# Layer 1's rows by scatter and its weights awaited apart; layer 0's index table in one-pass products

## The reference

```python
logits = xf @ W_router + expert_bias
top_vals, top_idx = jax.lax.top_k(logits, K_ACTIVE)
rw = jax.nn.softmax(top_vals, axis=-1)
g_r = silu(xf @ Wg_r[e]); u_r = xf @ Wu_r[e]
out_e = (g_r * u_r) @ Wd_r[e]
out = shared_out + sum_e combine[:, e] * out_e
```

## Time and profile before

| | |
|---|---|
| median of 3 runs | 1096.08 us (1094.7 to 1098.9) |
| profiled execution, its own time | 1098.63 us |
| its span, first to last instruction | 1096.5 us |
| PE busy | 92% of the span |
| mean granted clock of PE, of 2.4 GHz | 0.978 |
| routing of layer 0, from the logits' transposes to the first gate/up products | 338.1 to 363.8 us |
| routed blocks of layer 0, first gate/up to last down | 363.8 to 522.0 us |
| shared products of layer 1 | 704.3 to 759.3 us |
| routed blocks of layer 1, first gate/up to last down | 760.6 to 1061.3 us |
| shared down products | 1061.3 to 1092.3 us |

### The profile page before, as it was taken

One profiled execution on the slowest core, in us unless ns is written; L12 is line 12 of the kernel. 1 busy time (PEld: TensorE's weight loads), 2 busy tenths in 40 slices (PEclk: granted clock), 3 DMA queues, 4 the chain that ended last, 5 costly groups with the idle time before them and its releaser, 6 DMA issues.

```text
span 1096.5 us, 13333 instructions
## 1 busy us (share of the span) xinstructions
PE 1014.0 (92%) x4501; PEld 593.7 (54%) x4502; DVE 527.2 (48%) x934; ACT 323.0 (29%) x482; POOL 384.8 (35%) x333
## 2 busy tenths in 40 slices
PE   6998999999995799999598899999999999999998
PEld 3755555555453466665456555586544554555554
DVE  4466687887576255554565776851111111111114
ACT  2524545554631122221325554511111111111100
POOL 5514676767630222221524775311011111111014
PEclk9999999999997799999799999999999999999999
DMA  4679508000047176411434202503144444410015
GB/s 140 154 233 311 120 1 192 1 1 1 1 142 261 40 264 233 144 57 44 122 101 114 58 2 102 216 4 121 56 158 158 158 172 158 153 33 29 15 34 161
DMA packets 49722, 122.42 MB, mean 112 GB/s; under 512 B 6657, under 2 KB 23945, under 8 KB 49416
## 3 DMA queue, kind: packets, MB, share of 16 engines
q1 hardware_dynamic: 41224, 96.31, 27.8%
q0 software_dynamic: 8448, 25.44, 7.3%
HBM read 87.78 MB, written 22.94 MB: 101 GB/s over the span
## 4 chain that ended last, share of the span: by engine, by line
PE 75%; DVE 11%; DMA 6%; ACT 3%; issue 3%; POOL 1%; SPq 0%; DVEq 0%; ACTq 0%; POOLq 0%
PE PS L1863 22%; PE PS L1884 10%; PE PS L1644 5%; PE PS L1695 5%; PE PS L1554 5%; PE PS L1834 5%; DMA Wd<-in_Wd_r 5%; DVE nmax_part L1256 3%; PE PS L1676 3%; PE PS L1783 3%; PE PS L1910 3%; PE PS L1678 3%; DVE exp_acc L1288 2%; PE PS L1872 2%; DVE nmax L1256 2%
## 5 line engine op out<-in xcount | busy, mean ns | idle before, releaser
L1863 PE MATMUL PS<-Wgu,xbT 128*128 x690 | 287.5, 559 | 10.2 <-DMA Wd<-in_Wd_r 6.5
L1863 PEld LDWEIGHTS PS<-Wgu,xbT 128*128 128x128 f32 x690 | 128.6, 192 | 129.9 <-issue 117.2
L1056 ACT ACTIVATE expS<-PS 128x1024 f32<-128x1024 f32 (+3 forms) x156 | 135.6, 878 | 117.2 <-PE PS L1678 116.0
L953 POOL DMA_DIRECT2D block_rows_out<-yb x46 | 26.5, 576 | 388.2 <-DVE yb L1486 265.7
L1884 PE MATMUL PS<-Wd,hidT 128*128 x414 | 142.5, 490 | 1.5 <-DVE hidT L1448 0.8
L882 POOL TENSOR_TENSOR exp_acc<-exp_acc,expS 128x512 f32<-128x512 f32 (+1 forms) x65 | 124.7, 1918 | 47.3 <-ACT expS L1056 46.6
L1256 DVE TENSOR_REDUCE nmax_part<-PS 128x1 f32<-128x512 f32 x160 | 103.7, 685 | 44.7 <-PE PS L1644 44.0
L1676 PE MATMUL PS<-QA,KS 128*128 128x512 f32 (+3 forms) x312 | 114.3, 372 | 5.5 <-ACT QB L1034 4.8
L1644 PE MATMUL PS<-KS,QA 128*128 128x512 f32 (+2 forms) x288 | 109.5, 425 | 10.0 <-DVE nmax L1256 5.1
L1678 PE MATMUL PS<-QB,KS 128*128 128x512 f32 (+3 forms) x312 | 109.8, 358 | 0.0
L1884 PEld LDWEIGHTS PS<-Wd,hidT 128*128 128x128 f32 x414 | 78.4, 191 | 57.1 <-issue 13.4
(11 more groups left out here) (175 smaller groups left out, 1230.3 us busy)
## 6 DMA issues: line engine op xcount, KB each, us to landing
Wgu<-in_Wgu SPq DMA_DIRECT2D x8, 1152.0 KB, 5.7
Wgu<-in_Wg_r SPq DMA_DIRECT2D x8, 1152.0 KB, 5.8
Wgu<-in_Wu_r SPq DMA_DIRECT2D x8, 1152.0 KB, 10.1
Wd<-in_Wd_r SPq DMA_DIRECT2D x8, 1152.0 KB, 12.6
block_rows_out<-yb POOLq DMA_DIRECT2D x46, 192.0 KB, 2.2
part_rows<-parts SPq DMA_DIRECT2D x2, 3072.0 KB, 17.0
Wd<-in_Wd SPq DMA_DIRECT2D x8, 576.0 KB, 7.5
QA<-part_rows SPq DMA_DIRECT2D x8, 512.0 KB, 13.6
```

The costliest lines, as they stand in the source:

```text
L1056: act.activation(exp_tile(layer, c, unit)[:, pair, :].rearrange("p (b n) -> p b n", b=2)[:, :, lo:hi], PS[:, 2 * pair:2 * pair + 2, lo:hi] ...
L1863: last = pe.matmul(PS[:, 3 * par + lo // BANK, 0:n], xbT[:, par, kc, :], Wgu[layer][:, bass.ds(s, 1), kc, lo:lo + n], start=kc == 0, stop= ...
```

## The change

In layer 0 the index table's operands become fp32r (24 block columns instead of 23), and 10, 24 and 14 identity products are put before `ranks()`, between it and `table()`, and behind `table()`.

In layer 1 the table, its comparisons and the row stores go. SP zeroes `xs`, 23 blocks of rows in HBM, at the start of the kernel from a zeroed tile `zero_src`, and waits for that before it places the first keys. When `row_i` is ready, POOL scatters each of the 8 token tiles twice into `xs` (16 indirect transfers), and SP loads the blocks from there and stores their outputs. The routed experts' weights move from SP to POOL, with one semaphore for gate and up and one for down: a slot's gate/up is loaded again when its last block's gate/up products are done (`gu_psum`), its down weights when its last block's output is (`y_dve`); PE waits for the two apart. `xb_in` and `y_stored` become one set for each layer. The hidden tiles of VectorE that stood behind the wait for the table follow in order. What the new functions hold of layer 0 (`gather_blocks`) is as before.

```diff
+zero_src = at("zero_src", [P, C], PARTS)
...
-low_hot = sb("low_hot", [P, TOP * NT, P])
-high_hot = sb("high_hot", [P, TOP * NT, ROUTED_BLOCKS])
+low_hot = sb("low_hot", [P, TOP * NT, P], F32R)
+high_hot = sb("high_hot", [P, TOP * NT, ROUTED_BLOCKS + 1], F32R)
...
+xs = nc.dram_tensor("block_rows_in", [ROUTED_BLOCKS * P, C], F32, kind="Internal").ap()
...
-W_LOAD = [16 * 4, 16 * 3]
-W_BEFORE = [0, E * W_LOAD[0]]
+W_LOAD = [16 * 4, 16 * 2]
...
+    sp.wait_ge(zero_ready, 1)
+    sp.dma_start(xs.rearrange("(b p) c -> p b c", p=P),
+                 zero_src[:, :].rearrange("p (a c) -> p a c", a=1).broadcast_to([P, ROUTED_BLOCKS, C])).then_inc(xs_zeroed, 16)
...
+    def routed_rows():
+        m = moes[1]
+        def load(b, place):
+            sp.dma_start(xb[:, place, :], xs[bass.ds(b * P, P), :]).then_inc(xb_in[1][place], 16)
+        def step(b, place, more):
+            if more >= 4:
+                sp.wait_ge(bT_psum, b + (m.blocks_before + 1))
+                load(b + 4, place)
+            sp.wait_ge(y_dve, b + (m.blocks_before + 1))
+            sp.dma_start(ys[bass.ds(b * P, P), :], yb[:, place % 2, :]).then_inc(y_stored[1][place % 2], 16)
+        sp.wait_ge(scattered, 16 * TOP * NT)
+        for b in range(4):
+            load(b, b)
+        all_blocks(sp, step)
...
+    sp.wait_ge(xs_zeroed, 16)
     place_same(KS[0][0][D:3 * D], key_rows[0], a_in[0])
...
-    load_weights(moes[1], [Wg_s, Wu_s], Wd_s, shared_gu[:, :, :], shared_d[:, :, :], shared_in)
-    expert(1, 0, 0)
-    store_rows(1, 0)
-    store_rows(1, 1)
-    arrived(1, 1)
-    sp.wait_ge(shared_psum, HALF * moes[1].IC)
-    expert(1, 1, 1)
-    later_experts(1)
+    for n, w in enumerate((Wg_s, Wu_s)):
+        sp.dma_start(shared_gu[:, :, n * moes[1].I:(n + 1) * moes[1].I],
+                     w.rearrange("(k p) n -> p k n", p=P)).then_inc(shared_in, 16)
+    sp.dma_start(shared_d[:, :, :], Wd_s.rearrange("(k p) n -> p k n", p=P)).then_inc(shared_in, 16)
+    routed_rows()
...
+    pool.memset(zero_src[:, :], 0.0).then_inc(zero_ready, 1)
...
+        def load_gate_up(e, slot):
+            for n, w in enumerate((Wg_r, Wu_r)):
+                pool.dma_start(Wgu[1][:, slot, :, n * m.I:(n + 1) * m.I],
+                               w[bass.ds(e, 1)].rearrange("a (k p) n -> p (a k) n", p=P)).then_inc(wgu_in, 16)
+        def load_down(e, slot):
+            pool.dma_start(Wd[1][:, slot], Wd_r[bass.ds(e, 1)].rearrange("a (k p) n -> p (a k) n", p=P)).then_inc(wd_in, 16)
+        def shared_low_parts():
+            load_gate_up(0, 0)
+            load_down(0, 0)
+            for f in range(m.IC):
+                pool.wait_ge(gu_hi_ready, f + 1)
+                pool.tensor_tensor(chunk_of(gu_lo, f), chunk_of(shared_gu, f), chunk_of(gu_hi, f).bitcast(F32),
+                                   ALU.subtract).then_inc(gu_lo_ready, 1)
+        def scatter_rows():
+            pool.wait_ge(rows_ready, 1)
+            pool.wait_ge(xs_zeroed, 16)
+            for k in range(TOP):
+                for t in range(NT):
+                    pool.indirect_dma_start(
+                        xs[:, :], bass.IndirectOffsetOnAxis(ap=row_i[:, k, t:t + 1], axis=0),
+                        Xn[:, t, :], None).then_inc(scattered, 16)
+        def expert_weights():
+            pool.wait_ge(wgu_in, W_LOAD[1])
+            pool.wait_ge(wd_in, 16)
+            pool.wait_ge(shared_psum, HALF * m.IC)
+            load_gate_up(1, 1)
+            load_down(1, 1)
+            pool.wait_ge(tables_ready, 2)
+            with pool.Fori(m.slots, E) as q:
+                done = pool.value_load(end_i[1][0:1, bass.ds(q, 1)], min_val=1, max_val=m.blocks)
+                pool.wait_ge(wgu_in, q * W_LOAD[1])
+                pool.wait_ge(gu_psum, done + m.blocks_before)
+                load_gate_up(q, q % m.slots)
+                pool.wait_ge(wd_in, q * 16)
+                pool.wait_ge(y_dve, done + m.blocks_before)
+                load_down(q, q % m.slots)
...
-        pool.wait_ge(normalised, normalised_before(BLOCKS * (layer + 1) - 1) + TAIL_CUTS)
-        pool.iota(iota_low[:, :], pattern=[[1, P]], base=0, channel_multiplier=0,
-                  allow_small_or_imprecise_dtypes=True).then_inc(low_ready, 1)
-        if layer:
...
-        def load(b):
-            pool.indirect_dma_start(
-                xb[:, b % 4, :], None, xn_rows[layer][:, :],
-                bass.IndirectOffsetOnAxis(ap=index[layer][:, b:b + 1], axis=0)).then_inc(xb_in[b % 4], 16)
-        pool.wait_ge(xn_stored, 16 * HALF * (layer + 1))
-        pool.wait_ge(index_ready, layer + 1)
-        for b in range(4):
-            load(b)
-        for b in range(m.blocks):
-            if b + 4 < m.blocks:
-                pool.wait_ge(bT_psum, m.blocks_before + b + 1)
-                load(b + 4)
-            pool.wait_ge(y_dve, m.blocks_before + b + 1)
-            pool.dma_start(ys[b * P:(b + 1) * P, :], yb[:, b % 2, :]).then_inc(y_stored[b % 2], 16)
+        if layer == 0:
+            gather_blocks()
+        else:
+            shared_low_parts()
+            scatter_rows()
+            expert_weights()
...
-        dve.tensor_copy(row_i[:, :, :], row_f[:, :, :])
...
+        last = dve.tensor_copy(row_i[:, :, :], row_f[:, :, :])
+        if layer:
+            last.then_inc(rows_ready, 1)
...
-        dve.wait_ge(table_psum, layer + 1)
-        dve.tensor_copy(index[layer][:, 0:nr], PS[:, 7, 2 * P:2 * P + nr]).then_inc(index_ready, 1)
+        if layer == 0:
+            dve.wait_ge(table_psum, 1)
+            dve.tensor_copy(index[:, 0:nr], PS[:, 7, 2 * P:2 * P + nr]).then_inc(index_ready, 1)
...
-                    pe.wait_ge(hot_ready, pairs // 4 * layer + n // 4 + 1)
-                last = pe.matmul(PS[:, 7, 2 * P:2 * P + m.blocks], low_hot[:, n, :], high_hot[:, n, :],
+                    pe.wait_ge(hot_ready, n // 4 + 1)
+                last = pe.matmul(PS[:, 7, 2 * P:2 * P + m.blocks + 1], low_hot[:, n, :], high_hot[:, n, :],
...
+            keep_busy(5, 10)
             ranks()
+            keep_busy(5, 24)
             table()
+            keep_busy(5, 14)
...
-                if n == 6:
-                    table()
...
-                pe.wait_ge(w_in, (q + 1) * W_LOAD[layer] + W_BEFORE[layer])
+                pe.wait_ge(wgu_in if layer else w_in, (q + 1) * W_LOAD[layer])
...
             pe.wait_ge(hT_copied, b * per + (per + layer * ROUTED_BLOCKS))
+            if layer:
+                pe.wait_ge(wd_in, (q + 1) * 16)
```

More of the change, by code:

```diff
@@ L165, in build @@
         token = sb("token", [P, NT])
-        index = [sb(f"index{n}", [P, 32], I32) for n in range(2)]
+        index = sb("index", [P, 32], I32)
         ord_f = sb("ord_f", [P, 32])
@@ L639, in expert @@
-            def expert(layer, e, slot):
-                one = lambda w: w[bass.ds(e, 1)].rearrange("a k n -> (a k) n")
[L642 to L646, removed]
@@ L661, in later_experts, with arrived, store_rows @@
+            def arrived(q):
+                sp.wait_ge(w_in, q * W_LOAD[0])
+            def store_rows(half):
+                ts = slice(NT // HALF * half, NT // HALF * (half + 1))
+                sp.wait_ge(xn_ready, NT + ts.stop)
+                sp.dma_start(xn_rows.rearrange("(t p) c -> p t c", p=P)[:, ts, :], Xn[:, ts, :]).then_inc(xn_stored, 16)
+            def later_experts():
+                m = moes[0]
+                sp.wait_ge(tables_ready, 1)
                 for q in range(m.slots, E):
-                    done = sp.value_load(end_i[layer][0:1, q:q + 1], min_val=1, max_val=m.blocks)
@@ L663, in later_experts @@
-                    arrived(layer, q)
+                    done = sp.value_load(end_i[0][0:1, q:q + 1], min_val=1, max_val=m.blocks)
+                    arrived(q)
                     sp.wait_ge(y_dve, done + m.blocks_before)
-                    expert(layer, q, q % m.slots)
+                    expert(q, q % m.slots)
+            def routed_rows():
[12 more added lines that the diff above has]
+                all_blocks(sp, step)
@@ L713, in _ @@
             sp.wait_ge(sums_psum, BLOCKS)
[L714 to L718 removed]
+            expert(0, 0)
+            store_rows(0)
+            arrived(1)
+            expert(1, 1)
+            store_rows(1)
             for q in (2, 3):
[L720 to L721 removed]
+                arrived(q)
+                expert(q, q)
             sp.wait_ge(const_stored, 16 * 4)
@@ L841, in _ @@
             for layer in range(2):
+                m = moes[layer]
                 if layer == 0:
@@ L1473, in hidden @@
                                              ALU.add, ALU.mult).then_inc(hid_done, 1)
-                def stored_before(b, par):
-                    return b * 8 + (layer * 16 * ((m.blocks + 1 - par) // 2) - 8 * par)
                 def copy_y(b, par):
@@ L1482, in copy_y @@
                     dve.wait_ge(y_psum, b + (o + 1))
-                    if layer or not (isinstance(b, int) and b < 2):
-                        dve.wait_ge(y_stored[par], stored_before(b, par))
```

(2 more changed lines are left out.)

112 lines of the change are left out of this document (56 added, 56 removed).

## The result

The kernel after takes 1078.0 us (median of 4 runs, 1075.1 to 1078.7) against 1095.4 for the kernel before on the same chip (4 runs, 1094.4 to 1098.9). The ratio is 0.9824, 95% interval 0.9801 to 0.9847: 17.4 us less by the medians, 19.9 from one profiled execution to the other (1098.63 and 1078.72 us, spans 1096.5 and 1077.1). The forecast was 1074.3, the range 1071 to 1084.

The account below looks back on a forecast made before the run. PE, busy for 92% of the span, was taken to bound the kernel. Gains of 7.25 (layer 0), 5.2 (layer 1's table) and 9.4 us (late weights) make 21.8, from the 1096.1 median: 1074.3 us, range 1071 to 1084.

Parts of the forecast that it names:

- Table in one pass: Layer 0's index table on PE: fp32r products take one record instead of two, gaining 3.8 us (3.5 to 4.1).
- that bound: Layer 0's table at 0.11 us a product, full clock: VectorE is last, issuing the block order before reading the table.
- Identity products: Layer 0's routing: filler keeps PE's clock full; ranks gain 0.55, transposes 0.4, first gate/up 2.7, overshoot costs 0.2 us.
- The bounds of 0 and 1.7 us: Overshoot of the 14 products behind layer 0's table past the gathered rows' arrival: expected 0.2 us, 1.7 at half clock.
- the 7.25 us of layer 0: Layer 0's total gain from one-pass table and identity products, between 2 and 9 us.
- the sum: Whole gain over both layers: 7.25 + 5.2 + 9.4 = 21.8 us.
- Layer 1's table: Layer 1's shared products: removing the table saves 3.48 us of PE and 1.71 us of half clock, 5.2 us.
- Late weights: Layer 1's routed blocks: earlier gate/up loads and separate waits remove the excess of four late loads, 9.4 us.
- POOL's loads are slow: Rival, layer 1's expert switches: weight loads from POOL still late, gain 12.4 us, 1083.7 us; chance 0.06.
- Scatters: Layer 1: 16 scatters on POOL, 0.98 us each with 0.30 between, hidden by 7 us of cover, cost zero.
- the rival: Layer 1's scatters come late: beyond 1.74 us each PE waits; at 3.5 us each 1102.5 us; chance 0.03.
- Zeroing: Kernel start: zeroing 23 blocks in HBM, 4.5 MB in 13.6 us, over before the keys are placed, cost zero.

Follow-up runs that it names:

- both late kernels: Kernel after with layer 1's gate/up loaded again only at the old expert's last output: PE waiting apart 1078.2 us, PE waiting for gate/up and down together 1083.7 us.
- the one with many more products: Kernel after with PE's joint weight wait and, at the layer boundary, nine identity products for six, three for two, three behind layer 1's first transposes: 1079.0 us (0.9819).
- late loads, awaited together: Kernel after with gate/up loaded again only at the last output and PE waiting for gate/up and down weights together, still from POOL's queue: 1083.7 us (0.9872).
- the first batch: Kernel after run again without edit, and layer 0's parts, beside the kernel before (1098.5 us): the unedited repeat took 1077.8 us, ratio 0.9826.
- the three weight kernels: Kernel after with layer 1's gate/up load early and awaited with down 1074.9 us, late and awaited apart 1078.2 us, late and awaited together 1083.7 us.
- the doubled scatters: Kernel after with all 16 layer 1 scatters issued a second time once the first landed, SP waiting for both: 1097.6 us (0.9992).

## Why the prediction was right, and what it missed

**Table in one pass** (said 3.8 us). Right in kind: 3.4 us alone, from 7.0 to 3.6. In the kernel after the table's records last 2.4 us, not 3.5, since the clock is full while it runs and VectorE's comparisons set the pace, and VectorE's block order is last, as said for that bound.

**Identity products** (0.55 + 0.4 + 2.7 - 0.2). Ranks, transposes and gate/up gained 0.45, 0.36 and 2.73 us. The clock fell behind the table and the 14 products lifted it, as said; the last ends at 358.1 and the rows are in at 358.17, so the overshoot is zero in this profile. It isn't always: in three of the nine profiles with this routing (both late kernels, and the one with many more products) the clock fell inside the table, about 1 us earlier, and stayed low for nearly 7 us instead of 3.4; the 28 records took about 6.0 us instead of 5.0, and the transposes started 1.1 us later, behind them and not behind the rows. The bounds of 0 and 1.7 us held. The kernel without them shows that the gate/up gain is theirs. With routing at -7.65 the 7.25 us of layer 0 were met, and 1.0 us more came at layer 0's last down products, which the sum had left out.

**Layer 1's table** (5.2 us): 5.25. **Late weights** (9.4 us): 9.0. The size was right and the reason only in part. I gave all of it to the gate/up load's earlier start and the split wait; each alone does it, so the pair isn't needed, and with neither 4.0 us still go with the exchange of queues: 2.5 us of shorter waits and 1.7 of a low clock that didn't come. My rival "POOL's loads are slow" met its opposite: they took 5.8, 8.1 and 6.8 us to land. The Trainium skill, "DMA: Bandwidth & Descriptors", section "Issuing engine by pattern", says that SP's and ScalarE's path "is generally faster"; for three loads issued together these traces disagree, 10.5 us to the last from POOL (late loads, awaited together) against 12.6 from SP (the kernel before), or 11.8 to 12.1 against 12.4 to 13.8 from the first issue. Whether the path or the other transfers on each queue make the difference wasn't tried.

**Scatters** (zero). Said 0.98 us and 0.30 between; the trace has 0.968 and 0.30 x15. The first was issued at 714.9, the first block was in at 739.2, PE turned to it at 748.5. Doubling them gave the rival its price: the slack of 9.3 us once used up, the rest of the delay came one to one in the one delay that was tried, plus 5.1 us of slower loading beside the weights that follow on POOL's queue.

**Zeroing** (zero): one transfer of 4416 KB in 15.9 us, issued at 10.35, over by 26.3; the key rows were placed at 33.06 instead of 32.58, and PE's first scores came at 65.0, earlier than before.

**What the sum left out** is the boundary: layer 0's routing was costed as if the rest stayed as it was. By the profiled executions the forecast was 1076.8 and the measured time 1078.7, and the boundary's +2.8 us and 0.8 us at the start are more than that miss; the 1.0 us at the last down products went the other way. The other 1.8 us of the 3.7 between forecast and median are the 2.5 us that I took off because the kernel before's profiled execution stood above the median of its three runs: the one of the kernel after stands only 0.7 above its own, and in the three batches the kernel before took 1097.3 to 1098.5 us. The change was 20.7 us in the first batch, near the 21.8 of the sum, and nearly all of the difference to 17.4 lies in the kernel before (1098.5 against 1095.4), not in the kernel after (1077.8 against 1078.0). I had taken from the identity products their whole 3.5 us; net of the boundary they are worth 1.9 us by the times.

The second fall at the boundary came in five of the six profiles that have the kernel after's routing and boundary (its own two and those of the three weight kernels, not that of the doubled scatters, 27.4), and in none of the four with fewer or no identity products in the routing (26.9 to 27.1, before among them). Nor did it come with the fp32 table and all the identity products (28.07). So the identity products alone don't decide it. What goes with it is where the first fall lies: in the four it began 10 to 11 us before the boundary's first identity product and was over 3.1 to 3.6 us behind it; with the fp32 table it was over 4.0 us behind it; in the six it was over only 5.0 to 5.7 us behind it. Why the clock should fall once more after that isn't known, and the doubled scatters, which rose as late, didn't fall.

## What to carry to other kernels

Price a stretch by the granted clock beside the chain: half of what layer 0 gained was the same work at the full clock, and filler products pay only where PE waits anyway; look for the next pause behind them, where the clock can take the gain back, and look at several executions, since the same kernel's clock falls at different places. Where a load is late at a change of buffer, an earlier trigger or a split wait is enough, and trying each alone tells which. Before moving work off an engine onto a queue, measure its slack to the consumer and what stands behind it on that queue.

## What the runs showed that I had not expected

- Weight loads of 1152 KB issued from POOL landed no later than SP's: three issued together took 6.0, 8.2 and 10.5 us from their own issues (late loads, awaited together) against 5.8, 10.1 and 12.6 in the kernel before.
- The clock at the layer boundary differs between kernels that differ only in the routing, 160 us earlier, and between executions of the same routing. Three identity products behind the first transposes and one behind the variance kept it up in the profile (boundary 26.95 instead of 29.82 us); sixteen, of them twelve in the earlier waits, kept it up too, with a boundary 1.6 to 1.8 us longer than that. The times show no gain from either.
- A one-pass product of 24 columns took 0.22 us at half clock (3.6 us for 16), and the two-pass one 0.44 (7.0 for 16).
- A transfer of 192 KB took 7.6 us beside three of 1152 KB, and 2.5 us alone.
